# A decoder layer on one core: attention's routing, scatters and V products reordered, and the experts' first loads moved into its tail

## The reference, cut to what matters

```python
x = x + mamba(layernorm(x))                      # x: 4 x 1024 x 256, f32
h = layernorm(x)                                 # attention over a context of 77 rows per batch
q = rope(h @ Wq.T + bq); k = ctx @ Wk.T + bk; v = ctx @ Wv.T + bv        # 16 heads of 16
x = x + softmax(q k^T / 4) v @ Wo.T + bo
h = layernorm(x)
w, sel = top_k(softmax(h @ gate_w.T), 2); w = w / sum(w)                 # 8 experts
x = x + sum over the 2 chosen e of w_e * (up_e(h) * gelu(gate_e(h))) @ down_e.T
```

## Time and profile before

| | us |
|---|---|
| median of 3 runs | 2091.55 (2085.13 to 2096.99) |
| the profiled execution | 2098.59 |
| its span | 2096.8 |
| maxima of the scores (1091), first to last | 932 to 1245 |
| last exponentials (961) to first expert matmul | 1247 to 1333 |
| experts, PE without a gap | 1333 to 2081 |

### The profile page before, as it was taken

The page is one execution under the profiler, slowest core; times in us unless marked ns, Lnnn a source line. Parts: engine busy times, 40 slices in busy tenths (PEclk is TensorE's granted clock), DMA queues, the critical chain, the costliest instruction groups (busy, mean ns, idle before and its releaser), DMA issues. The chain is left out here.

```text
span 2096.8 us, 29458 instructions
## 1 busy us (share of the span) xinstructions
PE 1888.3 (90%) x10630; PEld 1529.4 (73%) x10630; DVE 1171.4 (56%) x1784; ACT 1088.2 (52%) x2125; POOL 1099.6 (52%) x807
## 2 busy tenths in 40 slices
PE   6889999999999999888888884699999999999998
PEld 2667777777776777776655653588888888888897
DVE  4899898999899988856765663011111111111111
ACT  3898989898989898826655551111111111111111
POOL 1687878787878787736566653222223232322121
PEclk8999999999999999999998996799999999999999
DMA  4021211121211114000120010974444444343441
GB/s 123 27 62 41 61 51 61 51 62 51 62 51 62 41 62 119 13 25 30 41 50 23 21 41 20 346 231 138 113 139 111 141 111 141 108 144 106 138 149 16
DMA packets 98163, 177.27 MB, mean 85 GB/s; under 512 B 24227, under 2 KB 68643, under 8 KB 87764
## 3 DMA queue, kind: packets, MB, share of 16 engines
q1 hardware_dynamic: 82308, 156.63, 22.2%
q0 software_dynamic: 15712, 18.76, 5.5%
HBM read 152.88 MB, written 22.82 MB: 84 GB/s over the span
## 5 line engine op out<-in xcount | busy, mean ns | idle before, releaser
L318 POOL TENSOR_TENSOR m_hc_ring<-m_h_ring,m_c_bc 128x1024 f32<-128x1024 f32 x256 | 606.1, 2374 | 128.9 <-DVE m_h_ring L479 110.6
L1584 PE MATMUL e_ps<-e_xT,e_w 128*128 128x256 f32 (+1 forms) x2560 | 501.3, 357 | 0.8 <-ACT e_xT L1511 0.8
L1584 PEld LDWEIGHTS e_ps<-e_xT,e_w 128*128 128x128 f32 x2560 | 441.1, 191 | 51.4 <-issue 1.1
L1495 POOL DMA_INDIRECT out<-e_y,e_who x71 | 113.4, 1597 | 557.0 <-DVE e_y L1547 459.7
L570 PEld LDWEIGHTS m_ps<-m_ident,m_bxT 128*128 128x128 f32 x2048 | 235.2, 141 | 216.0 <-DVE m_h_ring L479 102.8
L363 ACT ACTIVATE m_a_ring<-m_delta,m_negA 128x512 f32<-128x512 f32 x512 | 365.7, 715 | 39.9 <-DVE m_h_ring L479 39.5
L570 PE MATMUL m_ps<-m_ident,m_bxT 128*128 128x128 f32 x2048 | 321.1, 280 | 67.5 <-DVE m_h_ring L479 61.9
L375 ACT ACTIVATE m_bxT<-m_uT,m_bT 128x512 f32<-128x512 f32 x512 | 364.0, 711 | 0.0
L1538 DVE TENSOR_TENSOR e_hT<-e_gact,e_ps 128x512 f32<-128x512 f32 x142 | 97.7, 688 | 462.3 <-ACT e_gact L1520 462.3
L479 DVE TENSOR_TENSOR_SCAN m_h_ring<-m_a_ring,m_carry,m_ps 128x512 f32<-128x512 f32 x256 | 316.6, 1266 | 27.8 <-ACT m_a_ring L363 13.2
L479 DVE TENSOR_TENSOR_SCAN m_h_ring<-m_a_ring,m_ps 128x512 f32<-128x512 f32 x256 | 303.6, 1207 | 35.3 <-PE m_ps L570 12.0
(11 more groups left out here) (192 smaller groups left out, 2070.7 us busy)
## 6 DMA issues: line engine op xcount, KB each, us to landing
e_w<-in_gate_up_w SPq DMA_DIRECT2D x80, 1024.0 KB, 6.9
m_c_bc<-c_rows SPq DMA_DIRECT2D x32, 1024.0 KB, 6.0
e_w<-in_down_w SPq DMA_DIRECT2D x8, 1024.0 KB
m_x_in<-in_x SPq DMA_DIRECT2D x8, 512.0 KB, 5.8
m_x_res<-in_x SPq DMA_DIRECT2D x8, 512.0 KB, 6.9
x<-m_x_res SPq DMA_DIRECT2D x8, 512.0 KB, 2.9
t_xa<-x SPq DMA_DIRECT2D x8, 512.0 KB
out<-t_xa SPq DMA_DIRECT2D x8, 512.0 KB, 2.9
```

The lines of the kernel that those rows point to most:

```text
L318: p.tensor_tensor(hc_ring[:, k % HC, :, :], h_ring[:, n % 2, e:e + 2, :], c_bc[:, n, :].unsqueeze(1).to_broadcast([P, 2, CT]), ALU.mult).t ...
L1495: nc.gpsimd.indirect_dma_start(out=out, out_offset=bass.IndirectOffsetOnAxis(ap=who[:, tile:tile + 1], axis=0), in_=y[:, s % 2, i, :], in_ ...
L1584: last = t.matmul(gu_bank(s, g, which)[:, f * wide:(f + 1) * wide], w1[:, s % W1_RING, c, lo:lo + P], xT[:, s % 2, c, 0:wide], start=(c == ...
```

## The change

`products(g)` takes the place of `units(g)` for `times_v` alone, one slot later. The jobs move: OUT from q = 5, 6 to q = 6, 7, and RK from q = 7 to q = 3 of the next chunk, behind NT 1 and ahead of LG. `choose` is cut into four parts and, with `share_out` and `place`, is given slots of its own. The scatters stand one in each slot, V is masked over five slots, and the second normalisation is applied by ACT instead of DVE, from a shift that DVE makes. The experts' buffers and semaphores are placed before attention, on the common memory map, so that SP can load w2 of expert 0 after the last scores, w1 of steps 0 and 1 once `tables` is written, and the records of steps 0 to 3 once the scatters have landed; `e_ident` is no longer fetched. Line numbers in the diff are not those of the rows below, which are of the kernel before.

```diff
-    FIRST, LAST = -2 * HT, TOTAL + 2 * HT + 1
+    FIRST, LAST = -2 * HT, TOTAL + 4 * HT
-    jobs_at = [[("XT", 0, 1), ("XT", 1, 1)], [("Q", 0, 1)], [("Q", 1, 1), ("NT", 0, -2)], [("NT", 1, -2)],
-               [("LG", 0, -2)], [("OUT", 0, -1)], [("OUT", 1, -1), ("QT", 0, 1)],
-               [("QT", 1, 1), ("RK", 0, -2)]]
+    jobs_at = [[("XT", 0, 1), ("XT", 1, 1)], [("Q", 0, 1)], [("Q", 1, 1), ("NT", 0, -2)],
+                [("NT", 1, -2), ("RK", 0, -3)], [("LG", 0, -2)], [], [("OUT", 0, -1), ("QT", 0, 1)],
+                [("OUT", 1, -1), ("QT", 1, 1)]]
+    CHOOSE_AT, SHARE_AT, PLACE_AT, GAP_AT, SCATTER_AT = (22, 22, 24, 24), 26, 27, 25, 28
+    def products(g):
+        half, at = g // TI, g % TI
+        found = [(half - 2, 3)] if at == 0 else [(half - 2, 4)] if at == 1 else \
+            [(half - 1, 0), (half - 1, 1)] if at == 2 else [(half - 1, 2)]
+        return [(h, u) for h, u in found if 0 <= h < HALVES]
+    MASK_AT = (2, 2, 6, 6, 7)
@@ keep_chunks (SP) @@
         for c in range(NC):
+            if c == NC - 1:
+                sp.wait_ge(s_done, TOTAL)
+                weights.load_w2(sp, 0)
             wait_emptied(sp, "OUT", c, 1)
...
+        sp.wait_ge(tabled, 3)
+        for r in range(W1_AHEAD):
+            weights.load_w1(sp, r)
+        sp.wait_ge(blanked, 16 * 3)
+        for n in range(2):
+            sp.wait_ge(scattered[n], 16 * NT)
+        for r in range(M_AHEAD):
+            weights.load_meta(sp, r)
         sp.wait_ge(x2_stored, 16 * NC)
         sp.wait_ge(xn2_kept, 16 * NC)
-        for n in range(2):
-            sp.wait_ge(scattered[n], 16 * NT)
@@ slot (POOL) @@
-            if q == 0 and 0 <= c - 3 < NC:
-                scatter(c - 3)
+            for n in range(2 * TI):
+                k = chunk_at(g, SCATTER_AT + n)
+                if k is not None:
+                    scatter(k, n)
@@ slot (ACT) @@
-            if g % TI == 1 and 0 <= g // TI - 2 < HALVES:
+            if g % TI == 2 and 0 <= g // TI - 2 < HALVES:
                 head_out(g // TI - 2)
+            if q == 1 and 0 <= c - 2 < NC:
...
+                apply(c - 2, xn2s[:, c % 2, :, :], nmr2, rstd2, nmr2_ready, xn2_ready)
@@ slot (DVE) @@
-            if q in (4, 5) and 0 <= c - 2 < NC:
-                choose(c - 2, q - 4)
-            if q == 7 and 0 <= c - 2 < NC:
-                share_out(c - 2)
-                place(c - 2)
-            if q == 1 and 0 <= c - 2 < NC:
...
-                apply(c - 2, xn2s[:, c % 2, :, :], mv2, rstd2, rstd2_ready, xn2_ready)
+            for part in range(4):
+                if chunk_at(g, CHOOSE_AT[part]) is not None:
+                    choose(chunk_at(g, CHOOSE_AT[part]), part)
+            if chunk_at(g, SHARE_AT) is not None:
+                share_out(chunk_at(g, SHARE_AT))
+            if chunk_at(g, PLACE_AT) is not None:
+                place(chunk_at(g, PLACE_AT))
+            if q == 0 and 0 <= c - 2 < NC:
+                shift(c - 2, nmr2, mv2, rstd2, rstd2_ready, nmr2_ready)
@@ slot (PE) @@
-            for h, u in units(g):
+            for h, u in products(g):
                 times_v(h, u)
@@ experts_phase (SP) @@
             for s in range(STEPS):
-                if s >= W1_RING:
-                    sp.wait_ge(gu_done, first_group[s - W1_RING + 1])
-                load_w1(sp, s, tables, gate_up_w, w1, w1_loaded)
-                if s == 0:
-                    for r in range(M_AHEAD):
-                        load_meta(r)
-                if s < E:
+                if s >= W1_AHEAD:
+                    if s >= W1_RING:
+                        sp.wait_ge(gu_done, first_group[s - W1_RING + 1])
+                    weights.load_w1(sp, s)
+                if 0 < s < E:
...
```

More of the change, by code:

```diff
@@ L69, in offsets @@
         at += width
-    for under, names in ATTENTION_MAP.items():
+    for under, names in [*ATTENTION_MAP.items(), *EXPERTS_MAP.items()]:
         at_name = found[under]
@@ L152, in mamba_phase @@
         ps = ctx.enter_context(nc.psum_tensor("m_ps", [P, 8, BANK], F32))
-        parts = attention(place, sem, ident, ps)
+        parts = attention(sem, ident, ps)
         Y, BX, J = 0, 4, 6
@@ L912, in rope, with scatter @@
             ins.then_inc(rope_step, 1)
[L914 to L920, removed]
-                        out=slots, out_offset=bass.IndirectOffsetOnAxis(ap=pos_u[:, c % 2, k, i:i + 1], axis=0),
-                        in_=rec[:, c * TI + i, k, :], in_offset=None).then_inc(scattered[c % 2], 16)
+        def scatter(c, n):
+            k, i = n // TI, n % TI
+            if n == 0:
+                pool.wait_ge(placed, c + 1)
+                if c == 0:
+                    pool.wait_ge(blanked, 16 * 3)
+            nc.gpsimd.indirect_dma_start(
+                out=slots, out_offset=bass.IndirectOffsetOnAxis(ap=pos_u[:, c % 2, k, i:i + 1], axis=0),
+                in_=rec[:, c * TI + i, k, :], in_offset=None).then_inc(scattered[c % 2], 16)
         def slot(g):
@@ L932, in slot @@
                 normalise(g - 1)
-            if 0 <= c + 1 < NC and q in (3, 4, 5):
-                for k in (2 * (q - 3), 2 * (q - 3) + 1):
-                    rope(c + 1, k)
+            if 0 <= c + 1 < NC:
+                for k in range(ROPE):
+                    if q == ROPE_AT[k]:
+                        rope(c + 1, k)
             if 0 <= c < NC and q == 1:
@@ L952, in root, with apply @@
             a.activation(rstd[:], rstd[:], ACT.Exp, scale=-0.5).then_inc(ready, 1)
+        def apply(c, out, nmr, rstd, nmr_ready, ready):
+            act.wait_ge(nmr_ready, c + 1)
+            for i in range(TI):
+                a.activation(out[:, i, :], xa[c % X_RING][:, i, :], ACT.Identity, bias=nmr[:, i:i + 1],
+                             scale=rstd[:, i:i + 1]).then_inc(ready, 1)
         def exps(g):
@@ L1250, in slot @@
                     apply(c + 2, xn, mv1, rstd1, rstd1_ready, xn_ready)
+            if q == 7 and 0 <= c - 1 < NC:
+                wait_emptied(dve, "OUT", c - 1, 1)
+                for i in range(TI):
+                    measure(c - 1, i, stats2, ln2)
+                spread(c - 1, stats2, mv2, rstd2, ln2)
+            for part in range(4):
[7 more added lines that the diff above has]
+                shift(c - 2, nmr2, mv2, rstd2, rstd2_ready, nmr2_ready)
             if g == LAST - 1:
@@ L1408, in experts_phase @@
+def experts_phase(nc, place, ident, weights, xn2, tables, out):
+    w1, w2, meta = weights.w1, weights.w2, weights.meta
+    w1_loaded, w2_loaded, meta_loaded = weights.w1_loaded, weights.w2_loaded, weights.meta_loaded
+    _, E, KF, D = w2.shape
+    F = KF * P
+    KD = D // P
+    X_RING = 4
+    TILES = 2 * PAIRS + SINGLES
+    chunks_of = [KF // 4 if len(tiles_of(s)) == 2 else KF // 2 for s in range(STEPS)]
     groups_of = [KF // n for n in chunks_of]
     first_group = [sum(groups_of[:s]) for s in range(STEPS + 1)]
-    loads_of = [sum(len(tiles_of[r]) for r in range(s % X_RING, s + 1, X_RING)) for s in range(STEPS)]
+    loads_of = [sum(len(tiles_of(r)) for r in range(s % X_RING, s + 1, X_RING)) for s in range(STEPS)]
```

212 lines of the change are left out of this document (116 added, 96 removed).

## The result

The changed kernel takes 2057.3 us (median of 4 runs, 2054.81 to 2057.95) against 2090.2 for the kernel before in the same comparison (2085.13 to 2096.99): a ratio of 0.9838, interval 0.9808 to 0.9868. It is faster, 7 us under the forecast of 2064.5 and inside its range. The profiled execution took 2057.14 us with a span of 2055.0, against 2096.8, so the two traces differ by 41.8 us where the medians differ by 33.

What follows compares the result with a forecast made beforehand. PE, busy 1888 of 2097 us, was taken to bound the kernel, through attention's idle time, its clock and the 80 us before the experts. Terms -14 - 9 - 6 + 5 + 2 + 3 - 8 = -27 gave 2064.5 us, range 2040 to 2085.

Steps and rivals of the forecast that it cites:

- Products one slot later, with spread scatters: In mid-attention, PE finds t_pT made a slot ago and scatters hold POOL only briefly: -14 us (8 to 16.8 saved).
- the ceiling of 16.8 us: In attention, PE's waits for the copy t_pT, taken as the most that later products and spread scatters could save.
- Jobs: In attention, moved jobs and the second normalisation leaving DVE shorten PE's 15.2 us of transpose waits: -9 us (5 to 15.2 saved).
- Clock: In attention, PE's low-clock stretches around the POOL holds, costing 9.0 us, mostly go: -6 us (0 to 9 saved).
- Wait of LG: In five chunks, LG waits until place has emptied the bank that RK now fills behind NT 1: +5 us.
- POOL's load: In attention slots q = 3 to 5, POOL falls behind by 2.1 us and can recover: +2 us (0 to 8).
- The rival in which POOL and DVE bind: In attention, POOL falls behind in q = 3 to 5, half the waits stay: -7 us, 2084.5; chance 16%.
- Tail: After attention, LG waits 2.0 us more behind chunk 6's moved rank, and ACT applies at half width: +3 us (1 to 5).
- Boundary: Between attention and experts, records load before the barrier, the gather starts 4.7 us earlier: -8 us (-5 to -10).
- The sign I named for it: At the boundary: experts starting about 6 us sooner after the last exponential, with records landed before the barrier.
- everything fits: Product waits, job waits and low clock go whole, LG costs nothing: -48 us, 2044; chance 22%.
- the fourth rival: In attention, scatters held by DVE's normalisation through the locked port make POOL's chunk 49 us: +28 us, 2120; chance 2%.

Runs made afterwards that it cites:

- experiment 1: The changed kernel with the products with V, and ACT's copy of the attention output, back in the slot of their transposes: 2080.26 us, ratio 0.9968.
- experiment 3: The changed kernel with both the products back in the slot of their transposes and a chunk's eight scatters together again: 2092.93 us, ratio 1.0006.
- experiment 5: The changed kernel with the second normalisation on DVE again, by the old instructions and without the shift: 2063.34 us, ratio 0.9889.
- experiment 2: The changed kernel with a chunk's eight scatters together again, at the start of the chunk four later, with one more tail slot: 2079.56 us, ratio 0.9966.
- experiment 4: The kernel before with only its scatters spread, one in each slot, and the tail slots this takes: 2080.01 us, ratio 0.9937.

## Why the prediction was right, point by point

The time was within the range and nearest to the forecast, but the terms did not come out as sized. Two errors went opposite ways: attention gave more than I took, the boundary less.

*Products one slot later, with spread scatters: -14, and what they did was about -34 (the clock, booked apart at -6, is in it).* The step that mis-sized it is the ceiling of 16.8 us: I took the named waits of one row for all there was to win. The waits did go whole. What the row can't hold is what hangs on them: the low clock, DVE's instructions behind and beside POOL's, and PE's own busy time. And with the other parts of the change in place the row itself is larger, 24 us (experiments 1 and 3). Cut exactly at its transposes, the undisturbed chunk before is 34.92 us busy, one after 34.38, at the same clock of 1.00 (my 35.3 to 35.6 had up to 0.7 us of the next chunk in it). Length, then the columns of the earlier trace rows:

```profile
1005.40:1044.70 39.30, 34.92 (x171) 24.52 (x171) 29.45 (x79) 24.28 (x87) 22.20 (x21) 1.00 0.13 41
```

```profile
1074.67:1111.15 36.48, 34.38 (x170) 24.52 (x171) 27.98 (x78) 26.05 (x91) 27.54 (x23) 1.00 0.15 44
```

A stop costs more than the idle time that it shows, as two pairs of product matmuls in the timeline of before tell, one that follows on and one behind a wait:

```profile
1014.72 1.02 PE L1360 MATMUL m_ps<-t_pT,t_v_all 128*128 128x512 f32 x2
...
1019.55 1.13 PE L1360 MATMUL m_ps<-t_pT,t_v_all 128*128 128x512 f32 x2 [0.99 <-ACT t_pT L970]
```

That is 0.1 us a stop, some 0.5 us a chunk. Of the 19.2 us less of busy time the clock is some 9, this some 4 and the work behind the mark some 3 (all three estimates from these windows); the last 3 stay open. "Both work on the same 16.8 us" was half right: they overlap by some 10 us (experiment 3), but on waits of different kinds.

*Jobs: -9.* The waits for `t_q` and OUT's evacuation are gone or small (0.3 us for `t_xa` in the chunks). XT waits for ACT instead, 3.7 us against 0.7, QT for POOL 3.8 against 1.2 and NT 1.1, so some 8 of the 15.2 us went and the size was right. But the jobs are not a saving of their own: without the later products and the spread scatters the whole rest of the change is worth zero in time (experiment 3). The products in the same slot then wait 24.6 us, more than the 16.8 of before, and the tail takes 6.3 us back. The normalisation on ACT, which I booked at nothing beyond the waits, is worth 5 to 6 us (experiment 5).

*Clock: -6.* In the profiled pair all 9 came; the six stretches are at 1.00, and no dip came back in the chunks. The burst alone brings some back (experiment 2), the many short waits of experiment 1 don't.

*Wait of LG: +5.* It did not come there: no wait in attention, one of 0.7 us in the tail. The bank's handover is paid by RK instead, 3.0 us in five waits in attention and 1.4 in two in the tail. I had priced the second handover of the bank (RK to LG) and not the one that the move also made, NT 1 to RK with only one product between. The size was near, the place was not.

*POOL's load: +2.* POOL is busy up to 30.4 us of 36.5; waits for `t_probs` are 4.4 us in four. The one of 2.8 is in the tail, where the kernel before has one of 2.2; the other three, 1.6 us, are new and what I had forecast. The rival in which POOL and DVE bind did not come.

*Tail: +3.* It was +1.0 from the last exponentials to `tables`, and yet the forecast's terms all came. OUT 1 to LG is 13.2 us before (1274.14 to 1287.32) and 14.4 after (1233.82 to 1248.18), but the two OUT 1 ran at different clocks:

```profile
1274.14 3.78 PE L1290 MATMUL m_ps<-t_wo,t_oT 128*128 128x256 f32 x8 [0.84 <-DVE t_xa L1216]
```

```profile
1233.82 1.99 PE L1347 MATMUL m_ps<-t_wo,t_oT 128*128 128x256 f32 x8 [0.78 <-DVE t_xa L1274]
```

From the end of OUT 1 it is 9.4 us before and 12.4 after: +0.9 until NT begins, +2.0 from NT's second half to LG. The forecast was right here, and the 2 us that cover it are the clock's.

*Boundary: -8, and it was -2.9.* This step failed. I let the gather begin 3.8 us after the barrier's old end and took w1 of two steps as landed by then, so as help; the scatters were to land as before. But SP sees them landed 6.5 us after the last has left POOL, behind 4 MB of w1, instead of 2.3 with w1 behind the barrier, and the barrier comes late with them. The sign I named for it, records landed before the barrier, is there, and yet the first gather is only 1.7 us sooner behind `tables` (1264.72 to 1281.40, against 1303.92 to 1322.33), where I took 4.7. Also, PE's wait of 8.3 us for the gather hardly fell (7.2 here, where I took 5, and 8.7 with w1 behind, where w1 goes out in the same microsecond). With w1 behind, the gather comes 7.2 us sooner and the boundary gives 6.5 to 6.8 of the 8 us.

*The sum.* -27 against -41.8 in the profiled pair and -33 in the medians. The profiled execution of before was 7 us over its median, as I had noted, and I made the sum against it. That the median came out only 7 us from the forecast is in part luck: in the profiled pair attention was mis-sized by 18 us (-22 against -40), and the boundary by 5 us the other way. For that pair "everything fits" was nearer (-48 against -41.8): its attention was right (-40), for other reasons than its own, and the boundary took the rest back. For the medians the forecast was (2064.5 against 2044, measured 2057.3).

*The rule on the shared port.* With one scatter beside DVE's work in every slot, the median is 1.008 us instead of 0.971, the most 1.166 instead of 1.159. The Trainium skill's rule (SBUF — State Buffer, "A bandwidth-pool intuition that's wrong") would have made some of them last about 3 us; no run here shows it, and the fourth rival falls. From issue to landing the scatters take a median of 3.2 us in attention and 2.9 in the tail, where DVE has little to do. The two engines do hold each other up in these traces, but the other way round: it is DVE's `t_at` that lasts up to 4.60 us beside POOL (experiment 2), and 0.85 us once in the kernel after. I had looked at one side of the pair only.

## What to carry to other kernels

A row of waits in the trace bounds what its removal brings neither from below nor from above. The 16.8 us hid costs that stand in no row of PE's waits, and the job waits, removed without the rest, brought nothing in sum. Two stalls that cover each other have to be removed together: undo each alone and both at once, and the three numbers (22, 22, 34.5) tell how they overlap. A burst of small work on a queue is worth spreading even where the queue's mean load is low, also for what the queue does to its neighbours while it catches up. A large load fetched early must not be issued just ahead of small transfers that the path waits for: bytes that nobody needs yet delay those that everybody does.

## What the runs showed of the hardware

The small transfers beside full DMA engines: records of 2 KB each take a median of 1.8 us to land with w1 behind the barrier, and 3.8 and 5.8 us in the two traces of the kernel as changed. The four w1 loads also held SP's queue, for 3.27 us in one of these traces and 6.40 in the other. Behind them SP still waited 5.6 and 2.4 us for the scatters, so it was the landing that ended last both times, and not the queue.

A wait of PE for ACT's copy with at most a job between is 0.7 to 0.9 us on average in three kernels (experiments 1, 3 and 4), hardly ever more once POOL's burst is gone. And PE's granted clock stayed at 1.00 with 24 us of such waits spread over the stage, but fell in the kernel with the scatters together, where PE waited 2.3 to 3.5 us four times. Length alone does not tell: in the kernel before the clock fell around waits of 2.7 us (1077), 3.1 us (1105) and 1.9 us (1149), and stayed up through one of 2.6 us (1232).

A small instruction of DVE that reads two tiles in SBUF (`t_at`, 128x64) lasted 0.22 us all eight times in the kernel before (with no POOL instruction beside it in the five chunks of attention), 0.85 to 1.76 us beside one or two multiplications of POOL's (the kernel after once, experiment 3 four times), and 3.46 to 4.60 us beside three to five of them in a row (experiment 2). In all nine cases it ended 0.1 us after one of them. The two instructions ahead of it, which read one input from PSUM, took 0.15 to 0.18 us beside the same multiplications.
